# Feed-forward part by pairs of sequences, with the second half's quantisation and two weight products moved

## The reference

```
def _act_quant(x):
    scale = 127.0 / clip(max(abs(x), axis=-1, keepdims=True), 1e-05)
    return clip(round(x * scale), -128.0, 127.0) / scale
def _bitlinear(x, w):
    return einsum('bsi,oi->bso', _act_quant(x), _weight_quant(w))
gate = silu(_bitlinear(x, w_gate))      # inner size 512
up   = _bitlinear(x, w_up)
out  = _bitlinear(gate * up, w_down)    # back to 128 features
```

## Time and profile before

| what | value |
|---|---|
| median of 3 runs | 190.67 us (190.41 to 191.7) |
| profiled execution | 190.32 us |
| its span, first to last instruction | 188.6 us |
| outside the span | 1.72 us |
| PE busy | 164.9 us, 87% of the span |
| DVE busy | 130.8 us, 69% |
| ACT busy | 83.0 us, 44% |
| POOL busy | 55.7 us, 30% |
| chain that ended last, by engine | PE 62%, DVE 22%, ACT 7%, DMA 3%, issue 3%, POOL 1% |

### The profile page before, as it was taken

How to read it: one execution, slowest core, us unless ns; L and a number is a source line. 1 busy time by engine, 2 the same in 40 slices (tenths; PEclk the granted TensorE clock), 3 DMA queues, 4 the chain that set the end, 5 groups by cost and what they waited for, 6 DMA issues and landing times.

```text
span 188.6 us, 3925 instructions
## 1 busy us (share of the span) xinstructions
PE 164.9 (87%) x1510; PEld 102.2 (54%) x1510; DVE 130.8 (69%) x368; ACT 83.0 (44%) x145; POOL 55.7 (30%) x90
## 2 busy tenths in 40 slices
PE   0478999999999998888697789979899999999992
PEld 0134556655555544557376667546466675665662
DVE  0698457488788888688988797662888595553552
ACT  2122655463564553777557641644322373122120
POOL 8651632637784822526022005200002000000000
PEclk9999999999999999999999999999999999999999
DMA  5985000000000000000000000000000000100001
GB/s 166 404 286 219 0 3 5 0 3 2 5 0 3 3 0 5 0 0 3 0 0 0 3 0 0 2 3 0 2 0 0 3 0 3 53 0 5 0 0 56
DMA packets 1747, 5.84 MB, mean 31 GB/s; under 512 B 192, under 2 KB 320, under 8 KB 1600
## 3 DMA queue, kind: packets, MB, share of 16 engines
q1 hardware_dynamic: 1008, 4.01, 5.7%
q10 hardware_dynamic: 720, 1.57, 2.3%
HBM read 5.06 MB, written 0.52 MB: 30 GB/s over the span
## 4 chain that ended last, share of the span: by engine, by line
PE 62%; DVE 22%; ACT 7%; DMA 3%; issue 3%; POOL 1%; SPq 0%; DVEq 0%
PE bank L1303 9%; PE bank L1285 8%; PE bank L1288 8%; PE bank L1072 7%; DVE bank L701 5%; PE bank L1064 3%; DMA x_all<-in_x 3%; PE bank L1118 3%; PE bank L1296 2%; PE bank L1191 2%; PE bank L1121 2%; PE bank L1081 2%; ACT ffn_work L498 2%; ACT f_hqT L504 2%; PE bank L1004 2%
## 5 line engine op out<-in xcount | busy, mean ns | idle before, releaser
L701 DVE TENSOR_REDUCE bank<-bank 128x4 f32<-128x512 f32 x32 | 22.3, 696 | 13.5 <-PE bank L1072 12.4
L282 POOL TENSOR_SCALAR_AFFINE_SELECT pT<-pT 128x512 f32<-128x512 f32 x32 | 19.8, 644 | 25.8 <-ACT pT L427 25.7
L956 DVE TENSOR_TENSOR xnT<-full,bank 128x512 f32<-128x512 f32 x20 | 13.7, 683 | 17.9 <-PE bank L1288 15.3
L1303 PEld LDWEIGHTS bank<-ews,rest 128*128 128x128 f32 x160 | 20.7, 191 | 9.3 <-issue 5.3
L592 ACT ACTIVATE full<-bank 128x512 f32<-128x512 f32 x20 | 11.7, 596 | 29.2 <-PE bank L1285 29.2
L1303 PE MATMUL bank<-ews,rest 128*128 128x128 f32 x160 | 21.5, 277 | 1.9 <-DVE rest L961 1.9
L427 ACT ACTIVATE pT<-bank 128x512 f32<-128x512 f32 x32 | 17.4, 595 | 10.0 <-PE bank L1102 10.0
L1285 PE MATMUL bank<-nT,ews 128*128 128x512 f32 x40 | 20.7, 598 | 0.0
L1288 PE MATMUL bank<-nT,ews 128*128 128x512 f32 x40 | 20.4, 592 | 0.0
L1081 PE MATMUL bank<-qm,kT 32*128 32x512 f32 x64 | 18.0, 640 | 0.0
L1191 PE MATMUL bank<-maskb,identb 128*128 128x256 bf16 x128 | 17.1, 273 | 0.0
(11 more groups left out here) (169 smaller groups left out, 300.1 us busy)
## 6 DMA issues: line engine op xcount, KB each, us to landing
ews<-in_ew SPq DMA_DIRECT2D x1, 1928.5 KB, 7.4
fws<-in_fw SPq DMA_DIRECT2D x1, 768.0 KB, 8.2
cT<-in_ctxT ACTq DMA_DIRECT2D x2, 256.0 KB, 5.2
x_all<-in_x SPq DMA_DIRECT2D x2, 256.0 KB, 4.8
out_x<-x_all SPq DMA_DIRECT2D x2, 256.0 KB, 2.0
lws<-in_lw ACTq DMA_DIRECT2D x1, 449.0 KB, 8.5
sels<-in_sel ACTq DMA_DIRECT2D x1, 320.0 KB, 8.8
a<-in_aw ACTq DMA_DIRECT2D x1, 256.0 KB, 5.1
```

Of the source, the lines that this page charges most:

```text
L282: nc.gpsimd.affine_select(out=probs, in_=probs, compare_op=ALU.is_ge, fill=0.0, base=0, pattern=[[0, HG], [1, S]], channel_multiplier=-1). ...
L701: V.tensor_reduce(group_max(j // 2)[:, j % 2, :], bank[j][:, :].rearrange("p (h k) -> p h k", h=4), AX.X, ALU.max).then_inc(sm["a_mx"], 1)
L1303: last = mm(bank[6 + s][:, b * D:(b + 1) * D], e_h[:, u, b * S:(b + 1) * S], expert(c)[2], start=(c == 0 and b == 0), stop=(c == NC - 1), ...
```

## The change

Four things are done, and the arithmetic stays the same.

1. **Pairs.** DVE multiplies gate by up for two sequences, and then takes both maxima in one instruction over 2 x 512 columns, and the clip, reciprocal and factor for two in one instruction each (`pair_scales`). `f_h` has four slots in place of two. `down` of both sequences of a pair writes one bank (bank 6), and DVE adds them when both are there (`pair_residual`). The transposes of sequences 1 and 3 go through bank 7, so that they needn't wait for the copy of the sequence before; sequences 4 to 7 still share bank 5.
2. **Second half's input.** `x_quantize(1)` now comes after pair 1's scales and pair 0's residuals on DVE; its transposes on PE come after `down(3)`, where they came before `h_transposes(2)`.
3. **Weight products.** `keys_times_queries(1)` and `values_times_outputs(1)` go from the first four sequences to behind `down(7)`, with their copies on ACT behind `hT_copy(7)`; `values_times_outputs(0)` goes to just before `gate_up(4)`. The last three of the four products use bank 7, and those of half 1 wait for `residual3(0)`, which reads it.
4. **Fills.** The counts of `keep_busy` are changed; the last, before `x4_transposes(0)`, from 26 to 14, all together from 128 to 110. `gate_up(2)` and `gate_up(3)` come one after the other, and so do 4 and 5.

No transfer is added, removed or moved, and POOL's list stays as it is.

```diff
-        f_h = kxf[:, 3 * B * D:4 * B * D].rearrange("p (u n) -> p u n", u=2)
+        f_h = sb("f_h", [128, 4, INNER])
...
-        J_RAW, J_KQ, J_VO = 8, 10, 12
+        J_RAW, J_KQ, J_VO = 8, (10, 12), (11, 13)
...
+        def hT_bank(n):
+
+            return bank[7 if n % 2 and n < HALF else 5]
...
             def hidden_scale(n):
                 u = n % 2
-                act.wait_ge(sm["f_hstep"], STEPS2 * n + 3)
+                act.wait_ge(sm["f_hstep"], STEPS2 * (n // 2) + 3)
...
ACT's list, from the first silu to the copy of the router's input:
             kq_copy(0)
-            kq_copy(1)
+            silu(2)
+            silu(3)
             hidden_scale(0)
-            silu(2)
-            vo_copy(0)
             hidden_scale(1)
-            silu(3)
             hT_copy(0)
-            vo_copy(1)
+            hT_copy(1)
             hidden_scale(2)
-            hT_copy(1)
-
-
+            hidden_scale(3)
+            hT_copy(2)
+            hT_copy(3)
             xqT_copy(1)
             act.wait_ge(sm["f_deqr"], 4)
             silu(4)
-            hidden_scale(3)
-            hT_copy(2)
             silu(5)
-            hT_copy(3)
+            vo_copy(0)
+            silu(6)
+            xT3_copy(0)
+            silu(7)
+
+            nc.scalar.activation(table[:, 1:2], tg[:, 0:1], ACT.Exp)
             hidden_scale(4)
-            silu(6)
+            exp3(0)
             hidden_scale(5)
             hT_copy(4)
-            xT3_copy(0)
-            silu(7)
-
-            nc.scalar.activation(table[:, 1:2], tg[:, 0:1], ACT.Exp)
+            hT_copy(5)
+            pT3_copy(0)
             hidden_scale(6)
-            hT_copy(5)
-            exp3(0)
+            hidden_scale(7)
             hT_copy(6)
-            pT3_copy(0)
-            hidden_scale(7)
             hT_copy(7)
+            kq_copy(1)
+            vo_copy(1)
             xT4_copy(0)
...
DVE:
+            def pair_scales(i):
+
+                ns, at = slice(2 * i, 2 * i + 2), STEPS2 * i
+                dve.wait_ge(sm["f_hr"], 2 * i + 2)
+                V.tensor_reduce(f_ah[:, ns, 0], f_h[:, 2 * i % 4:2 * i % 4 + 2, :], AX.X, ALU.max,
                                 apply_absolute_value=True).then_inc(sm["f_hstep"], 1)
...
+            gate_times_up(0)
+            gate_times_up(1)
+            pair_scales(0)
             residual(B - 1)
             layer_stats(B - 1, 1)
             aggregate(1, 1)
-            ffn(1, False)
-            ffn(2, True)
+            gate_times_up(2)
+            gate_times_up(3)
+            pair_scales(1)
+            pair_residual(0)
             x_quantize(1)
-            ffn(3, True)
...
+            pair_residual(1)
             aggregate(2, 0)
-            ffn(5, False)
+            gate_times_up(4)
+            gate_times_up(5)
             layer1_normalize(2, n3, 0, "n3r")
-            ffn(6, True)
+            pair_scales(2)
+            gate_times_up(6)
             softmax3_args(0)
-            ffn_residual(5)
-            ffn_stats(5)
+            gate_times_up(7)
             softmax3_normalize(0)
-            ffn(7, False)
...
+            pair_scales(3)
+            pair_residual(2)
             residual3(0)
-            ffn_residual(7)
-            ffn_stats(7)
+            pair_residual(3)
             aggregate(2, 1)
...
PE's list after the change, from gate_up(3) on (waits left out where they are those of the helpers):
+            gate_up(3)
             keep_busy(0, 8)
             h_transposes(0)
+            keep_busy(0, 4)
+            h_transposes(1)
+            keep_busy(0, 4)
             down(0)
             down(1)
+            keep_busy(0, 14)
             h_transposes(2)
+            keep_busy(0, 4)
             h_transposes(3)
             keep_busy(0, 4)
             down(2)
             down(3)
+            xq_transposes(1)
+            values_times_outputs(0)
...
             gate_up(4)
+            gate_up(5)
             scores3_bias(0)
             gate_up(6)
+            pe.wait_ge(sm["proj_out"], J_VO[0] + 1)
+            x3_transposes(0)
...
+            keep_busy(2, 5)
+            scores3(0)
+            gate_up(7)
             pe.wait_ge(sm["f_silr"], B - 1)
+            keep_busy(1, 6)
             h_transposes(4)
+            keep_busy(1, 6)
+            h_transposes(5)
             down(4)
             down(5)
+            keep_busy(1, 8)
             p3_transposes(0)
             keep_busy(1, 5)
             y3_proj(0)
             keep_busy(1, 5)
+            h_transposes(6)
+            keep_busy(1, 6)
             h_transposes(7)
+            keep_busy(1, 4)
+            down(6)
             down(7)
+            keys_times_queries(1)
+            values_times_outputs(1)
             pe.wait_ge(sm["f_silr"], B)
-            keep_busy(2, 26)
+            keep_busy(2, 14)
             x4_transposes(0)
```

More of the change, by code:

```diff
@@ L115, in build @@
         fq = sb("fq", [128, 3, INNER], BF16)
-        kxf = sb("ffn_work", [128, 5 * B * D])
+        kxf = sb("ffn_work", [128, 4 * B * D])
         f_xn = kxf[:, 0:B * D]
@@ L189, in job_bank @@
         def job_bank(m):
-            if m >= J_KQ:
-                return bank[0 if m % 2 else 5]
+            if m >= J_KQ[0]:
+                return bank[0 if m == J_KQ[0] else 7]
             return bank[4 + m % 2]
@@ L503, in hT_copy @@
                 act.wait_ge(sm["f_hTp"], n + 1)
-                nc.scalar.activation(f_hqT[:, u, :], bank[5][:, :], ACT.Identity,
+                nc.scalar.activation(f_hqT[:, u, :], hT_bank(n)[:, :], ACT.Identity,
                                      bias=magic[:, 1:2]).then_inc(sm["f_hTs"], 1)
@@ L807, in ffn @@
                     .then_inc(sm["f_hstep"], 1)
[L808 to L814 removed]
+                dve.wait_ge(sm["f_hstep"], at + 2)
@@ L817, in layer1_normalize, with pair_residual @@
+                V.reciprocal(f_ah[:, ns, 2], f_ah[:, ns, 1]).then_inc(sm["f_hstep"], 1)
+                V.tensor_scalar(f_ah[:, ns, 3], f_ah[:, ns, 1], fdown[:, 0:1], None, ALU.mult).then_inc(sm["f_hstep"], 1)
+            def pair_residual(i):
+                for n in (2 * i, 2 * i + 1):
+                    ffn_residual(n)
+                for n in (2 * i, 2 * i + 1):
+                    ffn_stats(n)
             def layer1_normalize(r, dst, s, done):
@@ L1205, in h_transposes @@
                 pe.wait_ge(sm["f_htr"], n + 1)
-                if n >= 1:
+                if n == 1:
+                    pe.wait_ge(sm["a_res"], B)
+                elif n >= HALF:
                     pe.wait_ge(sm["f_hTs"], n)
+                elif n >= 2:
+                    pe.wait_ge(sm["f_hTs"], n - 1)
                 for c in range(4):
-                    last = nc.tensor.transpose(bank[5][:, c * S:(c + 1) * S],
+                    last = nc.tensor.transpose(hT_bank(n)[:, c * S:(c + 1) * S],
                                                f_ht[:, u, c * 128:(c + 1) * 128], ident)
@@ L1216, in down @@
                 pe.wait_ge(sm["f_hTs"], n + 1)
-                if n >= HALF:
+                if n >= 2 and n % 2 == 0:
                     pe.wait_ge(sm["f_res"], n)
-                elif n >= 2:
-                    pe.wait_ge(sm["f_res"], n - 1)
                 for c in range(4):
-                    last = mm(down_bank(n)[:, 0:D], f_hqT[:, u, c * S:(c + 1) * S], fq[:, 2, c * D:(c + 1) * D],
+                    last = mm(bank[6][:, u * D:(u + 1) * D], f_hqT[:, u, c * S:(c + 1) * S], fq[:, 2, c * D:(c + 1) * D],
                               start=(c == 0), stop=(c == 3))
```

111 lines of the change are left out of this document (35 added, 76 removed).

## The result

The kernel before takes 191.70 us (median of 11 runs, 190.19 to 192.6), the changed one 193.44 (11 runs, 192.31 to 196.66). The ratio is 1.0087, 95% interval 1.0049 to 1.0125: slower by 1.7 us. (Medians are of all executions, while ratios leave out those over 1.5% above the fastest of their kernel: 195.82 and 196.66 here, 218.0 in r5, of which r5's profile was taken, and in r10 five of the nine in which the clock fell.) The prediction was wrong: 193.44 lies above its range of 189.3 to 192.2, and where it said +0.1 the difference is +1.7. It had taken 190.67, the median of the first three runs, for the kernel before; with more runs that is 191.7.

What follows compares the result with a forecast made beforehand. The stretch was taken as bound by results handed between engines, no engine being full. Terms of -1.06 before and +1.25 behind `down(7)`, taken as +0.1, gave 190.4 for the profiled execution, 190.8 for the median; range 189.3 to 192.2.

Steps and rivals of the forecast that it cites:

- rival B: PE's clock falls after a 2.2 us pause before `h_transposes(4)`: +2.4, total 193.1 (191.6 to 194.7), chance 0.14.
- the sum: -1.06 before `down(7)` and +1.25 behind it: +0.2 if PE alone decided, +0.06 with `n4`, taken as +0.1.
- The lead before `down(7)`: Second half up to `down(7)`: `n3` 3.7 us ahead, shrinking until `down(7)` comes at 111.77 against 112.83, 1.06 ahead.
- a handing from ACT to PE: Allowance for passing a result from one engine to another: 0.03 to 0.11 us.
- the check on the old order: Old order reckoned the same way from 80.3: transposes at 116.04 against 116.31 read, 0.3 short over 36 us.
- Behind `down(7)`: Late products, their copy and 14 fills before the router's transposes: 4.32 us against 3.07, 1.25 more, none covered.
- That `n4` would be ready over 1 us earlier than its transposes: End of the stretch: `n4` ready at 114.67, then waiting 1.4 us for PE, with transposes at 116.10.
- Pairs on DVE: Scales for two sequences take 3.07 us against 3.76, 0.7 less per pair, 2.8 over four; maximum 1.22.
- rival C: DVE's maximum for two costs as a strided one, 2.0 instead of 1.22: +0.8, total 191.6, chance 0.03.
- rival D: DVE's saving arrives whole: 2.8 us come out, total 187.9, chance 0.06.

Runs made afterwards that it cites:

- r5: Kernel before with the masking `q_masked(1, 3)` moved ahead of the statistics on DVE; 190.62 us, ratio 0.9937.
- r10: r5 without three groups of fills (5, 5 and 10) ahead of `h_transposes(6)`, `down(6)` and `p3_transposes(0)`; 192.61 us, ratio 1.0009.
- r6: Changed kernel with the masking `q_masked(1, 3)` moved as in r5; 192.87 us, ratio 1.0045.
- r7: r6 with 20 more fills ahead of `h_transposes(4)`, in PE's pause; 191.73 us, ratio 0.9992.
- r3: r2 with 20 more fills ahead of `h_transposes(4)`, in PE's pause; 193.38 us, ratio 1.0077.
- r11: r5 with only the two half-1 weight products moved behind `down(7)`, 14 fills there, 8 fills in each old place; 192.04 us, ratio 1.0032.
- r8: r4 with the masking moved as in r5 and `h_transposes(5)` and `(7)` through bank 2; 189.09 us, ratio 0.9859.
- r9: r8 with `gate_up(7)`, `silu(7)` and `hidden_scale(5)` earlier, so the exponential's table loads while ACT waits; 187.50 us, ratio 0.9803.
- r4: r2 with the two half-1 weight products moved into PE's pauses through bank 0, 26 fills behind `down(7)`; 191.32 us, ratio 0.9997.
- r2: Changed kernel with `q_masked(1, 1)` moved ahead of the statistics, not the masking that collides; 195.38 us, ratio 1.0184.

## Why the prediction was wrong, step by step

**What it compared with.** 190.67 was the median of three runs, two of which lie in the lower group of its times. The kernel before is at 191.7. That puts the forecast 1.0 too low. The trace shown had the row (masking 0.47, POOL's product 1.79 beside 1.51 elsewhere), and I didn't ask why one product of POOL was longer than its like. The profile of the kernel before happened to be of one of its faster executions, in which the masking took 0.47.

**The clock, rival B.** The step that failed first is that the sum has no term for PE's clock. The place and the length of the pause were right (2.13 us, 2.2 forecast), and so were the mechanism and the sign named for it, records of doubled length after it. The ground for putting it at nothing was that no pause of up to 0.8 was followed by slow records and that PE is mostly occupied afterwards. The former said nothing of a pause of 2.1, and what PE had to do afterwards didn't prevent the fall. The fills in the old order, which I had read only as work whose result nobody reads, were of use: r10 takes 20 of them away and loses 2.0 us. B's price was 2.4; in totals it is 1.14 (r6 against r7), in single profiles 0.62, 1.20 and 1.92 of the stretch, one below and two in the lower part of the 0.8 to 4.0 given. That B's 193.1 comes near the measured 193.44 is in part luck: its price was 1.3 too high and the time it started from 1.0 too low.

**The lead before `down(7)`.** Forecast 1.06, measured at full clock 0.65: `down(7)` starts its matmuls 32.2 us behind the first product in r3, 32.85 in the kernel before. One step that was mis-sized is the price of a handing from ACT to PE. I took 0.03 to 0.11, and 0.06 behind `down(7)`. Where PE stood waiting for ACT's result ahead of transposes or a product of 32-bit values, the rows show 0.14 to 0.15 (`hT_copy(6)` ends at 113.23, the transposes start at 113.37; `kq_copy(1)` ends at 116.72, the second product starts at 116.87). Two such stand on the way to `down(7)`, ahead of `h_transposes(5)` and `(7)`, and at 0.06 each they make some 0.2 of the 0.41. In the old order fills or other work covered most of these handings, so the check on the old order came out well and hardly tested them. The other 0.2 isn't assigned to a step: `n3` starts where it was reckoned (15.15 behind the first product against 15.1), but `h_transposes(4)` 0.3 to 0.4 late.

**Behind `down(7)`.** Forecast 4.32 against 3.07; measured 4.58 in r11 and in r3. The mechanism was right: no cover, one bank, product, copy, product in a row. The size was 0.26 short, spread over all its terms: 0.09 in the handing from `kq_copy(1)`, 0.07 in the issue of the second product (0.96 for 0.89), 0.06 between the first product's start and its copy (1.11 for 1.05), 0.03 in the fills and 0.01 in the copy. That `n4` would be ready over 1 us earlier than its transposes held, with 1.7.

**The sum.** Those two parts together make 0.41 + 0.26 = 0.7 of the 0.87 at full clock; the rest is the 0.2 that the prediction had before it took `n4` into account. Totals give 1.11 for the same difference (r7 against r5); 0.24 of it no profile assigns. With the clock's 1.14 this is the 2.25 that the sum put at 0.1. (The parts listed for a pair on DVE add up to 3.03, not 3.07, which changes nothing.)

**Pairs on DVE.** The maximum for two took 1.22, as interpolated from rows 6, and rival C falls. `n3` came 3.7 us earlier as forecast (15.15 behind the first product against 18.83). The saved time on DVE didn't arrive, as said against rival D. But r8 and r9 show that it could have: with three waits out of the way the same pairs take the stretch to 32.91.

**What the whole change was worth.** Without its two late products and the pause, the order by pairs is as fast as the old one (r4, ratio 0.9997), and 0.56 us shorter in the stretch. Late products cost 1.42 by medians and 1.50 in the stretch (r11), the clock 1.14 (r7). Together that exceeds the 2.25 of r6 by 0.3, roughly what the rest gave; r11 ran in another group, so this 0.3 is no firmer than that.

## What to carry to other kernels

Before an order is changed, ask of each idle stretch that PE gets how long it is beside the longest one that the old trace shows at full clock; filler matmuls in the old order can be what keeps the clock up (r10), so they are not slack to be used up without a test. Work that only has to be done "some time" belongs in an idle stretch of PE (r4), never between the last result of a stage and the next stage's first instruction. And when times of one program fall in two groups, look for the one record whose length differs from its like before comparing medians.

## What the runs showed of the hardware

- A DVE `TENSOR_SCALAR` (128x512, 32-bit, 0.47 us) and a POOL `TENSOR_TENSOR` (1.51 us) on SBUF hold each other up. With DVE's start 0.02 to 0.04 us ahead DVE was held up in all five profiles (1.82 to 1.84 us, 1.36 more, and it ended 0.28 to 0.3 us behind POOL's product); with 0.05 of lead, in the one profile of the kernel before, POOL was (1.79, which is 0.28 more). With 0.22 to 0.25 us of lead POOL's product took 1.68 or 1.69 and the masking 0.54 to 0.56 in all six profiles of kernels with that edit in which the masking was read. An earlier masking shows the same: in the changed kernel it starts at 45.97 us, 0.92 behind a product of POOL (45.05, 1.52 long), takes 0.88 and ends 0.28 behind it. The Trainium skill ("SBUF — State Buffer", "Who interferes with whom") describes this exclusive hold on a shared port, for whoever issues first; these rows agree, but starts 0.05 us apart don't tell who that was.
- PE's clock went to half after a pause of 2.1 us in an otherwise busy stretch, and in r10 with pauses of 0.80, 0.78 and 1.37 us, but not after 0.51 and 0.52 us around a product of 1.1. It stood at half for some 3.4 us in the changed kernel and r6, and for some 6.8 us in r2 and r10. It fell 0.2 us behind the end of the pause in the changed kernel, 0.7 us behind it in r2 and 2 us in r6, and in some executions of the same programs (five of twelve in r6, three of twelve in r10) it didn't fall at all.
